# Expert tiles of 256 rows, brought in by a transposing DMA as fp16 high and low halves

## What is computed

```python
xt = x.reshape(-1, D)                                  # 4096 rows of 128
scores = jax.nn.softmax(xt @ gate_w.T, axis=-1)        # 8 experts
topk_w, topk_idx = jax.lax.top_k(scores, TOP_K)        # 2 of 8
out = jnp.zeros_like(xt)
for e in range(E):
    we = jnp.sum(jnp.where(topk_idx == e, topk_w, 0.0), axis=-1)
    out = out + we[:, None] * _ffn(xt, w1[e], b1[e], w2[e], b2[e])
out = out + _ffn(xt, sw1, sb1, sw2, sb2)               # shared expert
# _ffn: gelu(x @ w1.T + b1) @ w2.T + b2, 128 -> 512 -> 128
```

## Time and profile before

| | us |
|---|---|
| median of 3 runs | 661.71 |
| the runs | 661.6, 661.71, 672.46 |
| the profiled execution | 655.45 |
| its span, first to last instruction | 654.2 |

### The profile page before, as it was taken

One profiled execution on the slowest core, in us unless ns is written; L12 is line 12 of the kernel. 1 busy time (PEld: TensorE's weight loads), 2 busy tenths in 40 slices (PEclk: granted clock), 3 DMA queues, 4 the chain that ended last, 5 costly groups with the idle time before them and its releaser, 6 DMA issues.

```text
span 654.2 us, 19174 instructions
## 1 busy us (share of the span) xinstructions
PE 518.7 (79%) x6278; PEld 346.0 (53%) x6339; DVE 471.5 (72%) x1336; ACT 384.5 (59%) x1056; POOL 400.9 (61%) x822
## 2 busy tenths in 40 slices
PE   2468998998989889897857867586699999999910
PEld 1134665565656546464524544355577777777700
DVE  3576876878689979665767868866477767767728
ACT  2104766777876775667655676481476776676700
POOL 4653646587777677668878776677044445444445
PEclk9655998998999999789986888797699999999965
DMA  6223322213120020000000000002122222222159
GB/s 170 82 62 84 99 75 77 80 40 97 35 65 5 6 88 11 27 10 19 20 17 21 18 17 14 21 26 74 42 60 59 58 64 57 63 55 63 39 150 247
DMA packets 47521, 37.88 MB, mean 58 GB/s; under 512 B 6959, under 2 KB 42805, under 8 KB 47428
## 3 DMA queue, kind: packets, MB, share of 16 engines
q1 hardware_dynamic: 42884, 28.18, 16.1%
q0 software_dynamic: 4320, 8.47, 3.9%
q10 hardware_dynamic: 224, 0.02, 0.0%
HBM read 23.24 MB, written 13.71 MB: 56 GB/s over the span
## 4 chain that ended last, share of the span: by engine, by line
PE 45%; DVE 17%; POOL 16%; ACT 9%; issue 7%; DMA 4%; SPq 2%; POOLq 0%; ACTq 0%; DVEq 0%
PE ps L592 6%; PE ps L580 5%; POOL scr_rows L1163 4%; PE ps L582 3%; PE ps L343 3%; PE ps L384 3%; PE ps L381 3%; PE ps L361 3%; PE ps L568 3%; PE ps L581 2%; DVE H L794 2%; PE ps L594 2%; ACT H L608 2%; PE ps L407 2%; ACT PT L644 2%
## 5 line engine op out<-in xcount | busy, mean ns | idle before, releaser
L1239 POOL DMA_INDIRECT scr_back<-ysb,XT x71 | 75.3, 1060 | 95.9 <-DVE ysb L1065 91.4
L756 ACT ACTIVATE g<-ps,b1c 128x128 f32<-128x128 f32 x284 | 81.3, 368 | 47.2 <-PE ps L582 44.3
L1045 DVE TENSOR_REDUCE mx<-ps 128x4 f32<-128x384 f32 x128 | 66.9, 550 | 19.2 <-PE ps L384 18.6
L644 ACT ACTIVATE PT<-ps 128x512 f32<-128x512 f32 x128 | 70.4, 597 | 16.2 <-PE ps L343 15.4
L1163 POOL DMA_INDIRECT scr_rows<-PAY,SL x64 | 69.0, 1078 | 15.4 <-issue 15.0
L580 PE MATMUL ps<-xT,w1h 128*128 128x128 f16 x284 | 62.5, 222 | 4.2 <-issue 3.4
L1059 DVE CAST gh<-g 128x512 f16<-128x512 f32 x71 | 31.6, 446 | 44.2 <-ACT g L756 44.0
L581 PE MATMUL ps<-xT,w1h 128*128 128x128 f16 x284 | 62.4, 222 | 0.0
L582 PE MATMUL ps<-xT,w1l 128*128 128x128 f16 x284 | 62.3, 221 | 0.0
L343 PE MATMUL ps<-QB,KS 97*128 97x256 f16 x256 | 52.7, 289 | 6.4 <-issue 4.3
L592 PE MATMUL ps<-w2c,gh 128*128 x284 | 55.7, 277 | 1.3 <-DVE gl L1060 1.0
(11 more groups left out here) (231 smaller groups left out, 1588.1 us busy)
## 6 DMA issues: line engine op xcount, KB each, us to landing
XT<-scr_rows SPq DMA_DIRECT2D x71, 65.0 KB, 1.9
stg<-in_w_t SPq DMA_DIRECT2D x18, 256.0 KB, 2.8
KS<-scr_heads SPq DMA_DIRECT2D x24, 128.0 KB, 2.5
QS<-scr_heads SPq DMA_DIRECT2D x24, 128.0 KB, 3.0
X<-in_src SPq DMA_DIRECT2D x8, 256.0 KB, 5.0
H<-scr_back SPq DMA_DIRECT2D x8, 256.0 KB, 5.2
YB<-scr_back SPq DMA_DIRECT2D x8, 256.0 KB, 5.3
out<-X SPq DMA_DIRECT2D x8, 256.0 KB, 3.1
```

The lines of the kernel that those rows point to most:

```text
L644: A.activation(PT[:, k % 2, hf, :], ST[hf][:], ACT.Exp).then_inc(a_exp, 1)
L756: z = A.activation(g32[:, i % 3, cs], bank("first", i)[:, cs], ACT.Gelu, bias=b1f[:, j:][:, bass.ds(e, 1)])
L1045: V.tensor_reduce(mx[:, n % 2, c, :], SM[c % 2][:, 0:384].rearrange("p (g k) -> p g k", g=4), AX.X, ALU.max).then_inc(v_max, 1)
L1239: G.indirect_dma_start(back_d, bass.IndirectOffsetOnAxis(ap=XT[:, i % NR, D + 1:D + 2], axis=0), ysb[:, i % NY, :], None, bounds_check=2 * ...
```

## The change

The tile becomes 256 rows (`TOKS`), and NTL falls from 71 to 39 tiles. The payload no longer holds fp32: in the same 512 bytes ACT writes the fp16 high half and POOL, after waiting for ACT, subtracts to write the low half. SP fetches a tile with two DMAs: a transposing one, which brings 256 rows of 256 two-byte values in as `xT` [128 features, high/low, 256 rows], and a small one for weight and row number, `XM`. The PE transpose, ACT's copy and DVE's low half of `x` go, as does ACT's share of the scaling. `first` has 12 matmuls of 256 columns in two PSUM banks, `second` 24 of 128 columns and two bias matmuls, for two groups c of 128 rows. Lags are now `first` 0, `first_rest` 1, `second` 2, `send` 3; buffers NR = 5 for `xT` and `XM`, NG = 2 for `g32`, `gh`, `gl`, NY = 3 for `ysb`. Each tile is scattered by two indirect DMAs. Padding rows double to 256 per expert.

```diff
-NR, NY = 10, 5
+NR, NY, NG = 5, 3, 2
...
+        XM = sb("XM", [P, NR, 2, 2], I32)
+        xT = sb("xT", [P, NR, 2, TOKS], F16)
+        g32 = sb("g32", [P, NG, 4 * TOKS])
+        gh = sb("gh", [P, NG, 4 * TOKS], F16)
+        gl = sb("gl", [P, NG, 4 * TOKS], F16)
+        ysb = sb("ysb", [P, NY, 2, D])
...
-        EXPERT_LAGS = ("scale", 5), ("turn_rest", 1), ("first_rest", 3), ("send", 5), ("turn", 0), ("first", 2), ("second", 4)
-        LAG = dict(EXPERT_LAGS)
+
+        LAG = dict(first=0, first_rest=1, second=2, send=3)
...
+            for step in range(NTL + 2):
                 i = tile_of(step, "first")
                 if i is not None:
                     if i % 8 == 0:
                         words[i // 8] = T.value_load(EID[0:1, i // 8:i // 8 + 1], min_val=0, max_val=2 ** 24 - 1)
                     e = columns[i] = T.snap(((words[i // 8] >> 3 * (i % 8)) & 7) * 2 * F)
-                    bk = hold(6 + i % 2, ("first", i))
-                    T.wait_ge(*freed("turn", i))
-                    for j in range(4):
-                        o = bk[:, 128 * j:128 * j + 128]
-                        wh = wflat1[0][:, 256 * j:][:, bass.ds(e, 256)].bitcast(F16)
-                        wl = wflat1[1][:, 256 * j:][:, bass.ds(e, 256)].bitcast(F16)
-                        T.matmul(o, wh, xT[:, i % 4, 0, :], start=True, stop=False)
-                        T.matmul(o, wh, xT[:, i % 4, 1, :], start=False, stop=False)
-                        t = T.matmul(o, wl, xT[:, i % 4, 0, :], start=False, stop=True)
-                    fill(t, "first", i)
+                    xhi, xlo = xT[:, i % NR, 0, :], xT[:, i % NR, 1, :]
+                    T.wait_ge(d_xt[i % NR], 16 * (i // NR + 1))
+                    for half in range(2):
+                        bk = hold(4 + 2 * (i % 2) + half, ("first", i, half))
+                        for jj in range(2):
+                            o = bk[:, TOKS * jj:TOKS * jj + TOKS]
+                            wh = wflat1[0][:, 256 * (2 * half + jj):][:, bass.ds(e, 256)].bitcast(F16)
+                            wl = wflat1[1][:, 256 * (2 * half + jj):][:, bass.ds(e, 256)].bitcast(F16)
+                            T.matmul(o, wh, xhi, start=True, stop=False)
+                            T.matmul(o, wh, xlo, start=False, stop=False)
+                            t = T.matmul(o, wl, xhi, start=False, stop=True)
+                        fill(t, "first", i, half)
                 i = tile_of(step, "second")
                 if i is not None:
                     e = T.snap(columns.pop(i) * 2)
                     bk = take("second", i)
-                    o = bk[:, 0:D]
-                    T.wait_ge(v_g, i + 1)
-                    for j in range(4):
-                        cs = slice(128 * j, 128 * j + 128)
-                        T.matmul(bk[:, 0:2 * D], gh[:, i % 3, cs], w2f[:, 4 * D * j:][:, bass.ds(e, 4 * D)].bitcast(F16),
-                                 start=(j == 0), stop=False, skip_group_check=True)
-                        T.matmul(o, gl[:, i % 3, cs], w2f[:, 4 * D * j:][:, bass.ds(e, 2 * D)].bitcast(F16), start=False,
-                                 stop=False, skip_group_check=True)
-                    fill(T.matmul(o, ones2[:], b2f[:, bass.ds(e >> 3, 2 * D)].bitcast(F16), start=False, stop=True,
-                                  skip_group_check=True), "second", i)
+                    T.wait_ge(v_g, 2 * i + 2)
+                    for c in range(2):
+                        o = bk[:, D * c:D * c + D]
+                        for j in range(4):
+                            cs = slice(TOKS * j + P * c, TOKS * j + P * c + P)
+                            wh = w2f[:, 4 * D * j:][:, bass.ds(e, 2 * D)].bitcast(F16)
+                            wl = w2f[:, 4 * D * j + 2 * D:][:, bass.ds(e, 2 * D)].bitcast(F16)
+                            T.matmul(o, gh[:, i % NG, cs], wh, start=(j == 0), stop=False)
+                            T.matmul(o, gh[:, i % NG, cs], wl, start=False, stop=False)
+                            T.matmul(o, gl[:, i % NG, cs], wh, start=False, stop=False)
+                        t = T.matmul(o, ones2[:], b2f[:, bass.ds(e >> 3, 2 * D)].bitcast(F16), start=False, stop=True)
+                    fill(t, "second", i)
...
-                    A.activation(PAY[:, u % 2].bitcast(F32)[:, :, :, 0:D],
+                    A.activation(PAY[:, u % 2].bitcast(F16)[:, :, :, 0:D],
                                  unit(H, u).unsqueeze(2).broadcast_to([P, 4, 2, D]), ACT.Copy).then_inc(a_pay, 1)
...
+            for i in range(NTL):
+                if i % 8 == 0:
+                    words[i // 8] = A.value_load(EID[0:1, i // 8:i // 8 + 1], min_val=0, max_val=2 ** 24 - 1)
+                e = A.snap(((words[i // 8] >> 3 * (i % 8)) & 7) * 4)
+                for half in range(2):
+                    if i >= NG:
+                        A.wait_ge(v_g, 2 * (i - NG) + half + 1)
+                    A.wait_ge(*full("first", i, half))
+                    for jj in range(2):
+                        j = 2 * half + jj
+                        z = A.activation(g32[:, i % NG, TOKS * j:TOKS * j + TOKS],
+                                         bank("first", i, half)[:, TOKS * jj:TOKS * jj + TOKS], ACT.Gelu,
                                          bias=b1f[:, j:][:, bass.ds(e, 1)])
-                    z.then_inc(frees("first", i), 1)
+                    z.then_inc(frees("first", i, half), 1)
...
+            for step in range(NTL + 3):
                 i = tile_of(step, "first_rest")
                 if i is not None:
-                    if i >= 3:
-                        V.wait_ge(*full("second", i - 3))
-                    V.wait_ge(*freed("first", i))
-                    V.wait_ge(s_dve, did(V.tensor_copy(gh[:, i % 3, :], g32[:, i % 3, :])))
-                    V.tensor_tensor(gl[:, i % 3, :], g32[:, i % 3, :], gh[:, i % 3, :], ALU.subtract).then_inc(v_g, 1)
+                    if i >= NG:
+                        V.wait_ge(*full("second", i - NG))
+                    for half in range(2):
+                        cs = slice(2 * TOKS * half, 2 * TOKS * half + 2 * TOKS)
+                        V.wait_ge(*freed("first", i, half))
+                        V.wait_ge(s_dve, did(V.tensor_copy(gh[:, i % NG, cs], g32[:, i % NG, cs])))
+                        V.tensor_tensor(gl[:, i % NG, cs], g32[:, i % NG, cs], gh[:, i % NG, cs],
+                                        ALU.subtract).then_inc(v_g, 1)
                 i = tile_of(step, "send")
                 if i is not None:
-                    y = ysb[:, i % NY, :]
-                    V.wait_ge(a_y, i + 1)
-                    V.scalar_tensor_tensor(y, bank("second", i)[:, D:2 * D], XT[:, i % NR, :].bitcast(F32)[:, D:D + 1], y,
-                                           ALU.mult, ALU.add).then_inc(frees("second", i), 1)
+                    V.wait_ge(*full("second", i))
+                    V.wait_ge(d_xm[i % NR], 16 * (i // NR + 1))
+                    if i >= NY:
+                        V.wait_ge(d_y[i % NY], 32 * (i // NY))
+                    V.tensor_tensor(ysb[:, i % NY], bank("second", i)[:, 0:2 * D].rearrange("p (c d) -> p c d", d=D),
+                                    XM[:, i % NR, :, 0:1].bitcast(F32).broadcast_to([P, 2, D]),
+                                    ALU.mult).then_inc(frees("second", i), 1)
...
-                    G.tensor_copy(PAY[:, u % 2, :, :, D + 1], TOK[:, 4 * u:4 * u + 4, :]).then_inc(p_tok, 1)
+                    G.tensor_copy(PAY[:, u % 2, :, :, D + 1], TOK[:, 4 * u:4 * u + 4, :])
+                    G.wait_ge(a_pay, u + 1)
+                    half = PAY[:, u % 2].bitcast(F16)
+                    G.tensor_tensor(half[:, :, :, D:2 * D], unit(H, u).unsqueeze(2).broadcast_to([P, 4, 2, D]),
+                                    half[:, :, :, 0:D], ALU.subtract).then_inc(p_tok, 1)
...
+                for c in range(2):
+                    G.indirect_dma_start(back_d, bass.IndirectOffsetOnAxis(ap=XM[:, i % NR, c, 1:2], axis=0),
+                                         ysb[:, i % NY, c, :], None, bounds_check=2 * NT * P - 1,
+                                         oob_is_err=False).then_inc(d_y[i % NY], 16)
...
-                    Y.wait_ge(a_xT, i - NR + 1)
-                    Y.wait_ge(d_y[(i - NR) % NY], 16 * ((i - NR) // NY + 1))
+                    Y.wait_ge(*full("first", i - NR, 1))
+                    Y.wait_ge(d_y[(i - NR) % NY], 32 * ((i - NR) // NY + 1))
                 r = Y.value_load(RWI[0:1, i:i + 1], min_val=0, max_val=8 * CAP)
-                Y.dma_start(XT[:, i % NR, :], rows_d[bass.ds(r, P), :]).then_inc(d_xt[i % NR], 16)
+                Y.dma_start_transpose(xT[:, i % NR], rows_d[bass.ds(r, TOKS), 0:D].bitcast(F16)).then_inc(d_xt[i % NR], 16)
+                Y.dma_start(XM[:, i % NR], rows_d[bass.ds(r, TOKS), D:D + 2].rearrange("(c p) w -> p c w", p=P)).then_inc(
+                    d_xm[i % NR], 16)
```

More of the change, by code:

```diff
@@ L25 @@
 KB = S + 64
-CAP = NT * P + P
+TOKS = 256
```

(21 more changed lines are left out.)

63 lines of the change are left out of this document (12 added, 51 removed).

## The result

| | before | after |
|---|---|---|
| median, us | 661.65 | 728.42 |
| lowest and highest, us | 660.57, 672.46 | 726.78, 734.07 |
| the profiled execution, us | 655.45 | 726.8 |
| its span, us | 654.2 | 725.5 |

The change makes the kernel slower: the ratio of after to before is 1.103, with a 95% interval of 1.095 to 1.111, a loss of 66.8 us by the medians. The forecast was 703 us with a range of 679 to 745, a loss of 41.4. So the direction holds, and some 25 us of the size have to be explained.

A forecast was written before the change was run, and what follows sets the result against it. Before, TensorE bounds the expert stage; after, the five-buffer ring's loop: 12 rounds of 4.0 + 7.9 + 3.5 = 184.8 us end the stage 34.4 later, plus 7 for payload, 41.4 on 661.7: 703 us, range 679 to 745.

The forecast's parts named there:

- the ring's loop: Expert stage: with five buffers, fetch(i) waits for tile i-5's scatter; three tiles take A + 7.9 + L, against 10.95 at PE's pace.
- A: PE's first and second layer for one 256-row tile: 3.65 us at full clock, taken as 4.0 for a lower clock.
- DVE, rest and send: DVE's link in the loop: both halves of rest(j+2), then send(j), with the reaction: 2.8 us.
- POOL and landing: Scatter link of the loop: POOL starts 0.79 us after DVE, second scatter 1.28 later, landing 2.24 after its start: 4.3 us.
- L: Transposing DMA's time from issue to landing in the loop: taken as 3.5 us, bounds 2.0 and 5.3; each microsecond costs 13 us.
- PE reacts: PE's delay between the fetch's landing and first(0): 0.1 us, added at the start of the expert stage.
- f = 7: Ahead of the expert stage: POOL's eight added payload subtractions, 2.3 us each, partly in idle time, cost 7 us; ends 2 and 15.
- Start and end: Expert stage outside the rounds: first(0) at 458.6 + L + 0.1, first(2) 3.2 us later, 13.0 from first(38) to the end.
- PE as the bound: Rival for the expert stage: the loop hides and PE stays the bound, 645 to 650 us; chance 0.05.
- The mild loop: Rival for the expert stage: the loop binds mildly, L below 2.5, 674 to 690 us; chance 0.17.
- The slow transposing DMA: Rival for SP's fetch: the transposing DMA is slow in issue or in flight, 735 us up, 788 at L = 10; chance 0.18.
- The other signs in the profile: Expert stage: PE about 75% busy, SP waiting for scatters at nearly every fetch, POOL issuing scatter pairs 1.28 us apart.

The follow-up runs named there:

- sending first: Kernel after with DVE's send put ahead of first_rest in the same step, five buffers and transposing DMA kept: 693.60 us, 1.054 to before.
- the idle load: Kernel after with ten buffers, PE reading the transposing DMA's data, plus a plain load per tile into a buffer nobody reads: 647.96 us, 0.986 to before.
- the kernel with fillers: Kernel after with five matmuls of 512 columns on PE ahead of each tile's wait for data, from tile 3 on: 715.45 us, 1.089 to before.
- the plain load: Kernel after, five buffers, transposing DMA replaced by a plain one of the same bytes, data not transposed: 719.53 us, 1.093 to before.

## Why the prediction was right, and where its terms were off

**What binds now: right.** The earlier trace rows gave PE as the bound of the stage and SP's waits as hidden. The forecast made the ring's loop the bound behind the change. The chain shows that loop link by link, PE waits 61.6 us for its last link, sending first takes 35 us off, and ten buffers take 80 us off (with the idle load), with the work of all engines as it was but for that load.

**The terms of the round.** All from the chain and DVE's timeline above:

| term | forecast | measured | from, to |
|---|---|---|---|
| A, two layers on PE | 4.0 | 5.79 | 548.83, 554.62 |
| DVE, rest and send | 2.8 | 2.61 | 554.62, 557.23 |
| POOL and landing | 4.3 | 4.29 | 557.23, 561.52 |
| SP | 0.8 | 0.74 | 561.52, 562.26 |
| L | 3.5 | 2.83 | 562.26, 565.09 |
| PE reacts | 0.1, once | 0.43 | 565.09, 565.52 |
| round | 15.4 | 16.69 | |

Three terms are right within 0.2 us, and L is inside its bounds on the low side (2.6 to 3.0 in the chain's other rounds). The term that was mis-sized is A: the step "I take A = 4.0 for 3.65" put it 1.79 us too low. Two errors stand in it, of opposite sign. At full clock A is 3.37 (the kernel with fillers), less than 3.65. And the clock costs far more than a tenth: in this kernel the first layer behind a wait runs at the lower level whole, 2.7 us for 12 matmuls (548.83 to 551.56) where at the higher level it takes 1.5 (569.84 to 571.33 with fillers), and the second still takes 3.1 for 1.9. The forecast took the mean clock of stretches in which PE was busy 66 to 81% and applied it to A. But the wait lies in the loop right ahead of A, so that it is just these instructions that meet the lower clock, while the mean over the stretch is raised by the tiles that follow without a wait. In part luck hid this: L was taken 0.67 too long, and with L = 2.83 the forecast's own sum would have been 694, further from the result. "PE reacts" was counted once, at the start, and belongs in each round, 0.43.

**The payload: the mechanism right, the size not.** POOL's line is 2.13 us x8, as forecast (2.3). f = 7 became 13 in the kernel that has it alone, and is part of the 18.4 us by which the first fetch is late in the profile of after. What was mis-sized is the discount: 1 us for units 0 to 3, nothing for unit 6, 1.2 for unit 7. ACT's payload copies, beside the earlier trace rows:

```profile
L724 ACT ACTIVATE PAY<-H x8: 1048/1058/1082, 185.6 to 442.1; 128x1024 f16<-128x1024 f32 x8
```

The first starts 2.5 us earlier than before, the last 16.1 later. Read at POOL's copy of the row number, which stands just ahead of the subtraction (start after less start before), the drift grows from unit 4 to 5, 5 to 6, 6 to 7 and from there to the first fetch by 2.1, 2.1, 2.2 and 2.4 us, about a full subtraction each, unit 6 with its idle time included. That this idle time was used up by what came late ahead of it is the likely reading, not a tested one. One profile tells this size only roughly: the earlier steps of the drift go up and down by 1 to 7 us, and the first fetch scatters over 17 us between kernels with this payload. The 13 us are from the timed kernel.

**Start and end.** The starts of the first layer of tile 2 and tile 38:

```profile
485.70 0.28 PE L579 MATMUL ps<-xT,w1h 128*128 128x256 f16 x1 [1.17 <-DMA xT<-scr_rows]
...
681.81 0.39 PE L579 MATMUL ps<-xT,w1h 128*128 128x256 f16 x1 [4.71 <-DMA xT<-scr_rows]
```

From the first fetch to tile 0 it is 2.9 us (forecast 3.6), from there to tile 2 5.7 (3.2), since tile 0's first layer ran at the lower level and tile 2 waited 1.2 us for its fetch. From tile 38 to the first load back it is 17.9 (13.0): the step on PE takes 5.9 at the lower clock for 3.65, and then POOL issues the scatters of three tiles one behind the other, 691.02 to 697.46, where the forecast had those of one.

**The sum, with measured terms.** 2.9 + 5.7 + 196.1 for the twelve rounds + 17.9 are 222.6, 52.4 more than before; with 13 for the payload 65.4, and 66.8 is the loss by the medians. The rounds average 16.34 for 15.4, 11.3 us in all. The first takes 14.3 us, the later ones mostly 16.6 to 17.1; in the one of the table 1.79 of A and 0.43 of PE's reaction are too few by the forecast, 0.67 of L and 0.26 of DVE and SP too many. So of the 25 us that were missing 11 are the rounds, in which A is the term that is short, 5 the end, 2.5 the first two tiles, 6 the payload, and the start takes 0.7 back.

**The rivals.** PE as the bound fell: 5.3 us per tile and PE 73% busy. The mild loop fell on A, not on L. The slow transposing DMA fell: L = 2.83, and with the plain load the round is only 1.5 shorter. As to what the pages made of L: the rule of the Trainium skill, "VectorE: DVE Perf Modes", section "The three transpose paths", led to an estimated 5.2 us for four blocks of 128x128 one after another; the trace does not agree, it has 2.83 for all four. The Trainium skill, "DMA: Bandwidth & Descriptors", section "Latency and other measured facts", led to an estimate of 2.5, and that is near 2.83. The other signs in the profile came about as announced: SP's waits for scatters (28 of the 34 fetches that can wait, not nearly all), POOL's pairs 1.43 apart (557.99 to 559.42; 1.28 to 1.29 in the six at the end; forecast 1.28), PE 73% busy (75%).

## What to carry to other kernels

A ring of buffers hides a latency only as long as its depth times the consumer's pace exceeds the whole way around, from fetch to the last use's landing; when a tile is enlarged and the number of buffers halved, write that way down as one sum before looking at engine times, and look first at the order in which an engine serves the loop's link and its other work. If the loop closes ahead of TensorE, price its matmuls at the lower clock from the first one behind the wait, not at the mean of the stretch: behind the waits of 4.5 to 5.2 us here that was right, behind one of 2.2 us (send first) the level fell only seven matmuls later. Work added to an engine that carries the chain part of the time should be priced near its full duration: here 13 of 17 us came through.

## What the runs showed of the hardware

- A transposing DMA of 256 x 256 two-byte values lands 2.83 us after its issue in the round shown, a plain one of the same bytes 2.15 to 2.3. But it takes SP 1.21 us to issue (up to 2.5), a plain one 0.38. Where SP issues three DMAs per tile, that and not the landing is the price: 3.44 us per tile on average, and a stage 13.7 us longer than with three plain ones.
- Idle PE costs twice: matmuls of 256 columns took 0.21 us behind a wait and 0.11 later. 180 useless matmuls of 512 columns (five in 1.19 us) made the kernel no slower, and by the ratios probably some 10 us faster.
- A kernel in which PE executes one instruction in 0.7 us for stretches, with nothing in the profile to wait for, became 35 us faster with an additional load (28 by the ratios, 21 in the stage). The gaps are worth looking for (groups whose idle time is put down to issue) before a time is explained by data or engines; their cause was not found.
